# Two of four corners scaled by ScalarE in a deformable convolution, and gathers without pacing

## What is computed

```
v1 = pad_x[n_idx, y1i, x1i]; v2 = pad_x[n_idx, y1i, x2i]
v3 = pad_x[n_idx, y2i, x1i]; v4 = pad_x[n_idx, y2i, x2i]
value = (hh*hw*v1 + hh*lw*v2 + lh*hw*v3 + lh*lw*v4) * mask
out = einsum('nhwkc,ock->nohw', value, dcn_w)      # 9 taps x 128 channels -> 128 channels
x = x + out
```

## Time and profile before

| | us |
|---|---|
| median of 3 runs | 7793.46 |
| lowest and highest | 7793.0, 7794.48 |
| span of the profiled execution | 7801.1 |
| finish of the first round starts | 217.00 |
| finish of the seventh round starts | 523.49 |
| finish of the last half round starts | 565.55 |

### The profile page before, as it was taken

One profiled execution on the slowest core, in us unless ns is written; L12 is line 12 of the kernel. 1 busy time (PEld: TensorE's weight loads), 2 busy tenths in 40 slices (PEclk: granted clock), 3 DMA queues, 4 the chain that ended last, 5 costly groups with the idle time before them and its releaser, 6 DMA issues. The chain is left out here.

```text
span 7801.1 us, 158574 instructions
## 1 busy us (share of the span) xinstructions
PE 7121.8 (91%) x61039; PEld 2135.5 (27%) x61039; DVE 4792.3 (61%) x12112; ACT 6803.0 (87%) x5386; POOL 1211.1 (16%) x1165
## 2 busy tenths in 40 slices
PE   5557999999999999999999999999999999999987
PEld 2552222222222222222222222222222222222224
DVE  6895545555556766666766767666764454454653
ACT  2327999999999999999999999999999999999851
POOL 1752211111111121111111121212100000000000
PEclk8778999999999999999999999999999999999987
DMA  6755646454545455454545455454523333332338
GB/s 219 214 158 125 143 111 142 105 139 108 135 114 131 111 142 133 103 140 111 141 108 129 111 141 124 121 131 115 135 70 93 77 89 75 78 95 65 95 95 251
DMA packets 1512155, 960.25 MB, mean 123 GB/s; under 512 B 315721, under 2 KB 1415433, under 8 KB 1510802
## 3 DMA queue, kind: packets, MB, share of 16 engines
q1 hardware_dynamic: 1418562, 646.15, 34.4%
q0 software_dynamic: 92880, 304.42, 14.1%
HBM read 404.07 MB, written 76.38 MB: 62 GB/s over the span
## 5 line engine op out<-in xcount | busy, mean ns | idle before, releaser
L1155 ACT ACTIVATE e<-sc 128x1536 f32<-128x1536 f32 x4192 | 5723.2, 1595 | 275.6 <-PE sc L1057 170.9
L1089 PE MATMUL acc<-e,v_cur 128*9 128x512 f32 x25152 | 3347.2, 601 | 49.1 <-DVE acc_sb L992 48.9
L1057 PE MATMUL sc<-b_unit,a_cur 32*128 32x512 f16 x14592 | 1924.2, 388 | 221.2 <-ACT e L1155 181.5
L1057 PEld LDWEIGHTS sc<-b_unit,a_cur 32*128 32x128 f16 x14592 | 474.5, 91 | 3422.2 <-ACT e L1155 2586.2
L1051 DVE STREAM_TRANSPOSE e_turned<-e_turned 128x1024 f32<-128x1024 f32 x896 | 1065.9, 1222 | 120.3 <-DMA e_turned<-e_kept 98.3
L1155 ACT ACTIVATE e_kept<-sc 128x1536 f32<-128x1536 f32 x672 | 953.8, 1538 | 65.5 <-PE sc L1057 40.5
L628 POOL DMA_INDIRECT room<-table,idx_st x432 | 491.4, 1138 | 2153.7 <-ACT e L1155 1647.2
L628 POOL DMA_INDIRECT corners<-table,idx_st x441 | 434.8, 986 | 2045.7 <-ACT e L1155 1633.1
L1089 PE MATMUL acc<-e_kept,v_cur 128*9 128x512 f32 x4032 | 701.9, 598 | 0.0
L1089 PEld LDWEIGHTS acc<-e,v_cur 128*9 128x9 f32 x25152 | 398.8, 88 | 833.2 <-issue 757.5
L1080 PE MATMUL acc<-e_turned,v_cur 128*9 128x256 f32 x7168 | 470.8, 380 | 0.0
(11 more groups left out here) (396 smaller groups left out, 5222.0 us busy)
## 6 DMA issues: line engine op xcount, KB each, us to landing
e_turned<-e_kept SPq DMA_DIRECT2D x3584, 128.0 KB
table<-pix SPq DMA_DIRECT2D x8, 2304.0 KB, 13.7
ew<-in_ew SPq DMA_DIRECT2D x12, 1024.0 KB, 7.7
ew<-in_ew SPq DMA_DIRECT2D x48, 256.0 KB, 6.6
x_ch<-in_x SPq DMA_DIRECT2D x4, 2048.0 KB, 10.1
qn<-q SPq DMA_DIRECT2D x64, 128.0 KB, 2.6
ctx<-ctx_t SPq DMA_DIRECT2D x128, 64.0 KB, 1.8
out<-e_exp SPq DMA_DIRECT2D x32, 256.0 KB, 2.1
```

What stands on the lines that cost most here:

```text
L1057: last = self.nc.tensor.matmul(self.sc[k % self.SC][:, i, :], self.a[rows, t * P:(t + 1) * P], self.bst[u % 2][rows, :], start=True, stop= ...
L1089: last = self.nc.tensor.matmul(self.acc[32 * h:32 * h + self.E1, :], self.v[:, t, h, :], src, start=(i == 0), stop=(i == self.UNIT - 1))
L1155: self.nc.scalar.activation(out, self.sc[k % self.SC][:], ACT.Exp, scale=1.0 / HD ** 0.5).then_inc(self.exp_done, 1)
```

## The change

ScalarE scales corner 1 into `cf_val_1` first, counts `cf_act_second`, then scales corner 0 into `cf_val_0` and counts `cf_act_val` as before. VectorE no longer waits for the turning of the tile two before it, but for `cf_act_second` of its own tile, and only adds corners 2 and 3. It has 18 instructions a tile in place of 27, ScalarE 18 in place of 9. The steps that VectorE counts in a sample are one fewer, so the bases of the counts change. The gathers lose their waits on VectorE's steps and keep the one on the indices.

```diff
-    ROUND_STEPS = 2 * W + FINISH_STEPS
-    S2 = ROUND_STEPS - 3
-    THIRD = [S2 + k // 3 for k in range(TAPS)]
-    NEXT_FIRST = [S2 + 3 + k // 3 for k in range(TAPS)]
-    FINISHING = [ROUND_STEPS + 3 + (FINISH_STEPS - 2) * k // (2 * TAPS) for k in range(2 * TAPS)]
...
-        def gather(i, j, at=None, ticks=(0,) * TAPS):
+        def gather(i, j):
             for k in range(TAPS):
                 if k == 0:
                     pool.wait_ge(idx_ready, i * W + j + 1)
-                if at is not None and (k == 0 or ticks[k] > ticks[k - 1]):
-                    pool.wait_ge(dv, at + ticks[k])
...
         def later(i, last=False):
-            at = (i - 2) * ROUND_STEPS + 2 * W
-            gather(i, 1, at, THIRD)
-            gather(i, 2, at, NEXT_FIRST)
-            gather(i, 3, at, FINISHING[:TAPS])
+            for j in range(1, W):
+                gather(i, j)
             if not last:
-                gather(i + 1, 0, at, FINISHING[TAPS:])
+                gather(i + 1, 0)
...
             dve.wait_ge(gathered[j], (i + 1) * (16 * TAPS))
-            dve.wait_ge(tr_full, (n + 1) * NG)
-            for c in (1, 2, 3):
+            dve.wait_ge(act_second, n + 1)
+            for c in (2, 3):
                 for k in range(TAPS):
                     src, wt, dst = corners[j][:, k, c * P:(c + 1) * P], w_st[j][:, k, c:c + 1], val[j % 2][1][:, k, :]
-                    if c == 1:
-                        last = v.tensor_scalar(dst, src, wt, None, ALU.mult)
-                    else:
-                        last = v.scalar_tensor_tensor(out=dst, in0=src, scalar=wt, in1=dst, op0=ALU.mult, op1=ALU.add)
+                    last = v.scalar_tensor_tensor(out=dst, in0=src, scalar=wt, in1=dst, op0=ALU.mult, op1=ALU.add)
                 if c < 3:
                     st.link(last)
             last.then_inc(val_ready, 1)
...
             act.wait_ge(tr_full, (n + 1) * NG)
-            for k in range(TAPS):
-                last = nc.scalar.activation(val[j % 2][0][:, k, :], corners[j][:, k, 0:P], ACT.Copy, scale=w_st[j][:, k, 0:1])
-            last.then_inc(act_val, 1)
+            for c, done in ((1, act_second), (0, act_val)):
+                for k in range(TAPS):
+                    last = nc.scalar.activation(val[j % 2][c][:, k, :], corners[j][:, k, c * P:(c + 1) * P], ACT.Copy, scale=w_st[j][:, k, c:c + 1])
+                last.then_inc(done, 1)
```

More of the change, by code:

```diff
@@ L396, in stage_conv_first @@
     ps_y = stack.enter_context(nc.psum_tensor("cf_ps_y", [P, 2, 512], F32))
-    dv, idx_ready, w_ready, act_val, val_ready, tr_full, tr_free, prod_done, x_in, t1_ready, q_ready, stored = (
-        sem("cf_" + n) for n in ("dve", "idx_ready", "w_ready", "act_val", "val_ready", "tr_full", "tr_free",
+    dv, idx_ready, w_ready, act_second, act_val, val_ready, tr_full, tr_free, prod_done, x_in, t1_ready, q_ready, stored = (
+        sem("cf_" + n) for n in ("dve", "idx_ready", "w_ready", "act_second", "act_val", "val_ready", "tr_full", "tr_free",
                                  "prod_done", "x_in", "t1_ready", "q_ready", "stored"))
@@ L518, in _ @@
         with dve.Fori(1, ROUNDS) as i:
-            st = Steps(dve, dv, (i - 1) * (2 * W + FINISH_STEPS) + 2 * W)
+            st = Steps(dve, dv, (i - 1) * (W + FINISH_STEPS) + W)
             sample(i, 0, st)
@@ L523, in _ @@
                 sample(i, j, st)
-        finish_last(ROUNDS - 1, Steps(dve, dv, (ROUNDS - 1) * (2 * W + FINISH_STEPS) + 2 * W))
+        finish_last(ROUNDS - 1, Steps(dve, dv, (ROUNDS - 1) * (W + FINISH_STEPS) + W))
     @block.scalar
```

## The result

The changed kernel takes 7817.84 us (median of 8 runs, 7809.5 to 7820.0), the kernel before 7796.45 in the same comparison (8 runs, 7793.0 to 7805.94). The ratio is 1.0027, interval 1.0017 to 1.0036: 21.4 us slower. The forecast was 7819, in a range of 7803 to 7832.

A forecast was written before the change was run, and what follows sets the result against it. No engine was taken as full; the bound was a path through finish, tile 1's sample, TensorE's turnings with ScalarE's copies, and corner 0. First round +6.1, six rounds +20.4, last -1.3: +25.2 on 7793.5 gives 7819 us, range 7803 to 7832.

The forecast's parts named there:

- The bound: First convolution's rounds: no engine is full; VectorE counts for 27.2 of 51.20 us, and only tile 1's sample is on the path.
- Tile 0's sample behind corner 0: Round's end: tile 0's additions wait for ScalarE's corner, queued behind tile 3's copies; corner to finish 8.43 us, not 3.32: +5.11.
- Tile 3's corner ahead of tile 2's copies: On ScalarE: corner grows from 2.74 to 5.37 us, delaying tile 2's first copy; +0.3 us a round, ends 0 and 1.2.
- The size of a round: Finish to finish: -2.01 (tile 1) + 0.3 (tile 3's corner) + 5.11 (tile 0) = +3.40, so 54.6 us; six rounds +20.4.
- The first round: Paced by gathers: corner 0 comes 2.63 us later, at 214.65, plus 8.43 gives first finish at 223.1, not 217.0: +6.1.
- The last round: Closing finish of half a round waits only for tile 3's sample: 40.75 us in place of 42.06, so -1.3.
- The gathers: GpSimd's gathers lose their waits on VectorE's steps: costed at nothing, idling about 9 us a round for buffers, median near 0.95.
- A: Rival, not slower: TensorE turns tile 1 at full clock, saving 2.57 us in each of seven turnings; 7801 us, chance 0.07.
- B: Rival, faster: VectorE is the bound and each of its samples shortens the time by 2.01 us; 7729 us, chance 0.05.
- C: Rival, slower still: unpaced gathers meet VectorE's additions and slow down, six rounds add 16 us; +41, 7835 us, chance 0.08.

The follow-up runs named there:

- a later kernel: Changed kernel with the next round's corner 0 ahead of tile 3's copies, plus identity products on TensorE ahead of tile 1's turning: 7770.59 us, ratio 0.9968 to the kernel before.
- the version with the early corner alone: Changed kernel with the next round's corner 0 ahead of tile 3's copies: ratio to the kernel before 0.9978 unpaced (7780.97 us), 0.9983 with gathers paced (7781.22 us).

## Why the prediction was right, step by step

**The number.** 7819 against 7817.84 is closer than the working deserves. The forecast was +25.2 us on 7793.5, the measured change is +21.4 on 7796.45: the sum was 4 us too large, and the kernel before came out 3 us slower in this comparison. The way and the mechanism are right, the agreement within 1 us is luck.

**The bound.** Right. VectorE lost 45 us of work in six rounds, and they took 16.6 us more. Only tile 1's sample was VectorE's own on the path.

**Tile 0's sample behind corner 0.** Right, and it is the cause: forecast 8.43 us from the corner to the finish, measured 8.24. The hand-over to the additions is short by the difference, 2.77 in place of 2.96. Taking this one tile back on chip A takes the 5.1 us a round away, and moving the corner ahead of the copies does so too, with all of ScalarE's work left in place.

**Tile 3's corner ahead of tile 2's copies.** The mechanism is there (the copy starts at 529.55, right at the corner's end), but from corner 3 to the next corner 0 it takes 13.77 us, and 13.67 before. The delay is 0.1, not 0.3. Tile 3's additions start at 527.12 after 2.98 of idle time (some 4 forecast; 2.98 to 4.46 in the six rounds) and are done before TensorE wants them at 533.35, so this cover held with a little over 1 us to spare, as reckoned.

**The size of a round.** Forecast 54.6, measured 53.85. The round shown, in the terms of the forecast: finish 19.80 for 20.14, additions 5.07 for 5.08, tile 1's turning until corner 3 5.96 for 6.98, then 13.77 for 13.97, and 8.24 for 8.43. The sum is 52.84. The round before it is 19.92, 5.07, 7.46, 13.77 and 8.24, 54.46 in all. What I took for fixed is tile 1's turning: it lasts 5.73 to 7.23 us in this kernel, and 6.53 to 6.86 in the one before. It starts at the lower clock each time, and its length is set by when the clock rises within it. In the turning of 5.73 us the granted clock is 0.50 until 521.0 and 1.00 from 521.5 on; in the one of 7.23 us, from 463.98, it is 0.50 until 470.0 and 1.00 from 470.5 on. What sets that moment isn't shown: both followed some 16 us of idle time. The term was over-sized by 0.2 to 0.3 for the finish, 0.2 each for the copy and the hand-over, and by what the turning happened to take.

**The first round.** Forecast +6.1, measured +6.2. Corner 0 starts at 214.94 (forecast 214.65), the finish 8.25 later.

**The last round.** Forecast -1.3, measured -2.0. The sum is thus 6.2 + 16.6 - 2.0 = 20.8 against a forecast of 25.2, nearly all of the difference in the six rounds.

**The gathers.** "At nothing" is right for the chip of the result and for chips A and B: GpSimd idles 6.4 us a round for buffers (forecast about 9), the median is 946 ns, and pacing makes no difference between two otherwise equal kernels (rounds of 48.0 us without it on chip A, 48.1 with it on chip B). It is wrong for chips C and D, where taking the pacing away costs 1.2%.

**The rivals.** A is false for this kernel: with 16.20 us of idle time the clock is 0.50 at the start of tile 1's turning. The gap is shorter than the 18.7 us that A reckoned with, since tile 0's turning ahead of it had itself slowed to 6.38 us. That turning started at 0.50 after only 5.70 us of idle time, which speaks against A more strongly than the 12.35 us that I had. Its price is of the right size: with the clock at 1.00 throughout the turning, a later kernel gains 1.9 us a round, where A had 2.57. B is false by chip A's -2.4 us a round for three tiles. How much of that is tile 1's alone isn't settled, since the kernel with only tile 1 on ScalarE ran on chips C and D alone. C is false as it was told: the gathers did not become slower beside VectorE's additions.
The Trainium skill, "GPSIMD Engine Reference", section "Key points", gives the contention on which C rested; the median of 946 ns in both kernels does not show it, while VectorE does the same 18 additions a tile in both, now unpaced. Single gathers take up to 1.40 us, against 1.29 before, but the mean from 217 to 546 us fell from 993 to 977 ns, so there is no stretch on the whole.

## What to carry to other kernels

Before work is moved to an idle engine, read where in that engine's order the moved piece will stand, and who is queued behind the wait that it makes. An idle engine whose next slot is late can be worse than a busy one: here the same work cost 5.1 us a round behind tile 3's copies and nothing ahead of them. Then look for the next bound before paying for more. Here it was TensorE's clock after a gap, and right behind that the issue of the gathers.

## What was not expected of the hardware

Two of four chips ran the kernel before 2.3% slower (7979 and 7982 against 7796 to 7799). On them engines came down to one instruction per 2 to 3 us, for long stretches, beside indirect gathers issued back to back, and ran freely once these had stopped. It is seen on TensorE (one record per 2.8 us), on VectorE (one pair per 2.1 to 2.8 us) and in ScalarE's waits. Pacing the gathers is worth 1.2% there (8077.65 against 7979.26, 8076.66 against 7982.19) and nothing on A and B, where it was tried on the version with the early corner alone. That the gathers cause it is likely by the pacing but not shown, and what differs between the chips is open.

In the changed kernel tile 1's turning (36 records, after 15 to 17 us of idle time) takes 5.73 to 7.23 us for the same instructions. It starts at the lower of the two clock levels (0.50) and ends at the higher (1.00), and the change came 3 us after its start in the shortest case and 6 us in the longest. It takes 4.18 to 4.28 where TensorE was at work just before it. Tile 0's turning of the changed kernel started at the lower level after 5.70 us of idle time.
